# Last cross attention of a four-layer gated stack: six weight units in a ring, value products in halves, an unused product behind each half

## What is computed

```
q = (input @ Wq + bq).reshape(b, tq, H, D).transpose(0, 2, 1, 3)
kv = (encoded_features @ Wkv + bkv).reshape(b, tk, 2, H, D).transpose(2, 0, 3, 1, 4)
scores = jnp.einsum('bhqd,bhkd->bhqk', q, k) / math.sqrt(D)
attn = jax.nn.softmax(scores, axis=2)
out = jnp.einsum('bhqk,bhkd->bhqd', attn, v)
out = out.transpose(0, 2, 1, 3).reshape(b, tq, H * D)
return out @ Wo + bo
```

## Time and profile before

| | |
|---|---|
| median of three runs | 1382.56 us |
| the three runs | 1377.02, 1382.56, 1384.98 us |
| profiled execution | 1379.09 us |
| its span on the core | 1377.3 us |
| granted TensorE clock, mean of the span | 0.965 |
| PE / PEld busy | 91% / 65% |
| DVE / ACT / POOL busy | 71% / 68% / 54% |
| stage of the change (first scores to end of L1860's first addition) | 1261.7 to 1341.3 us |

### The profile page before, as it was taken

How to read it: one execution, slowest core, us unless ns; L and a number is a source line. 1 busy time by engine, 2 the same in 40 slices (tenths; PEclk the granted TensorE clock), 3 DMA queues, 4 the chain that set the end, 5 groups by cost and what they waited for, 6 DMA issues and landing times. The chain is left out here.

```text
span 1377.3 us, 44922 instructions
## 1 busy us (share of the span) xinstructions
PE 1253.2 (91%) x17964; PEld 893.7 (65%) x17964; DVE 975.1 (71%) x2481; ACT 934.4 (68%) x2297; POOL 742.6 (54%) x749
## 2 busy tenths in 40 slices
PE   6999978999999999999999999999868798997767
PEld 4777635676766777667667766667656666765444
DVE  3666648888888888888887888888743544544566
ACT  5777746677777777777767777777656555554771
POOL 3444438888878887878877778778710001004000
PEclk9999989999999999999999999999998898999799
DMA  4000033222225223422342234222302000000000
GB/s 198 1 1 1 1 111 72 66 62 60 60 63 143 60 61 84 124 56 65 79 125 52 62 80 121 57 62 70 81 2 100 0 1 27 1 0 1 1 1 16
DMA packets 68319, 76.95 MB, mean 56 GB/s; under 512 B 14864, under 2 KB 62992, under 8 KB 67600
## 3 DMA queue, kind: packets, MB, share of 16 engines
q1 hardware_dynamic: 68112, 74.07, 20.2%
HBM read 26.31 MB, written 0.52 MB: 19 GB/s over the span
## 5 line engine op out<-in xcount | busy, mean ns | idle before, releaser
L1047 POOL TENSOR_TENSOR arena<-arena,small 128x512 f32<-128x512 f32 x96 | 100.2, 1044 | 149.2 <-DVE small L930 149.2
L795 ACT ACTIVATE arena<-banks 128x512 f32<-128x512 f32 x96 | 57.4, 598 | 143.6 <-PE banks L653 143.4
L906 DVE TENSOR_TENSOR arena<-banks,rotary 128x512 f32<-128x512 f32 x192 | 131.6, 685 | 31.5 <-ACT arena L765 18.7
L1022 POOL TENSOR_TENSOR arena<-arena 128x512 f32<-128x512 f32 x96 | 122.9, 1280 | 36.3 <-DVE arena L908 36.2
L702 PE MATMUL banks<-arena 64*64 64x32 f32 x6144 | 112.5, 221 | 17.1 <-issue 9.6
L1027 POOL TENSOR_TENSOR arena<-arena 128x512 f32<-128x512 f32 x96 | 122.8, 1279 | 2.2 <-DVE arena L908 2.2
L702 PEld LDWEIGHTS banks<-arena 64*64 64x64 f32 x6144 | 100.4, 135 | 28.6 <-ACT arena L817 11.9
L503 POOL TENSOR_TENSOR arena<-arena,small 128x512 f32<-128x512 f32 x64 | 66.6, 1041 | 86.9 <-DVE small L437 86.9
L616 PE MATMUL banks<-slot,z 128*128 128x512 f32 x192 | 101.4, 610 | 7.4 <-DVE z L996 3.4
L717 PE MATMUL banks<-arena,slot 128*128 128x128 f32 x768 | 104.2, 279 | 2.1 <-ACT arena L825 1.9
L1034 POOL TENSOR_TENSOR arena<-arena,small 128x512 f32<-128x512 f32 x96 | 100.7, 1049 | 1.8 <-ACT small L805 1.8
(11 more groups left out here) (308 smaller groups left out, 3310.2 us busy)
## 6 DMA issues: line engine op xcount, KB each, us to landing
arena<-arena SPq DMA_DIRECT2D x576, 64.0 KB, 2.0
slot<-in_pack_dram SPq DMA_DIRECT2D x28, 339.5 KB
arena<-arena SPq DMA_DIRECT2D x288, 32.0 KB, 1.8
slot<-in_pack_dram SPq DMA_DIRECT2D x2, 2713.5 KB
slot<-in_pack_dram SPq DMA_DIRECT2D x1, 3333.0 KB
slot<-in_pack_dram SPq DMA_DIRECT2D x1, 2316.5 KB
slot<-in_pack_dram SPq DMA_DIRECT2D x4, 337.0 KB
slot<-in_pack_dram SPq DMA_DIRECT2D x7, 158.0 KB
```

What stands on the lines that cost most here:

```text
L906: e.tensor_tensor(rot, made, cos, ALU.mult)
L1022: e.tensor_tensor(m.rot_q[u % ROTS], m.rot_q[u % ROTS], m.sin_q[u % 2], ALU.add).then_inc(s["q_added"], 1)
L1047: e.tensor_tensor(p, p, stretch(m.local_small[u % 4][:, 16:24], SPAN), ALU.subtract).then_inc(s["lowered"], 1)
```

## The change

The weights of a unit go to one of six buffers in `slot0` (`RING3` = 6, 1024 columns each), whose own contents are no longer needed. The values' products of a pair of units are cut in their two halves i: one half behind the scores of unit n, the other behind those of n+1, later than before (`LAG3` = 3, plus one). Behind every half stands one product of the identity with `m.x[0]`, full in shape (128 rows, 128 columns of weights, 256 columns wide), into bank 7; nothing reads it. The sums of all b share bank 6, b even on the left and b odd on the right, so the first half for a new b waits until ScalarE has copied out the b before (`s3_kept` at b). `act_found3` stands one unit earlier in ScalarE's program (`KEEP3` = 3). ScalarE's wait for a free weights buffer is now on the pair of six units before.

```
-LAG3, KEEP3 = 2, 4
+RING3, LAG3, KEEP3 = 6, 3, 3
...
-def weights3(m, b, w):
-    part = (m.t_w[b][:, 0:1024], m.t_w[b][:, 1024:2048], m.t_w[b][:, 2048:3072], m.t_v[b])[w % 4]
+def weights3(m, n):
+    part = m.slots[0][:, n % RING3 * 1024:(n % RING3 + 1) * 1024]
     return part.rearrange("p (g i q) -> p g i q", g=2, i=NT)
+
+
+def found3(m, b):
+    return m.bank[6][:, b % 2 * N:(b % 2 + 1) * N]
...
-    for n in range(UNITS3 + LAG3):
+    for n in range(UNITS3 + LAG3 + 1):
...
-        if n >= LAG3 and (n - LAG3) % 2:
-            b, j, pair, w = unit3_of(n - LAG3)
-            out, vz = m.bank[6 + b % 2][:, b // 2 * N:(b // 2 + 1) * N], expanded_values(m, b)
+        if n >= LAG3 + 1:
+            v = n - LAG3 - 1 - (n - LAG3 - 1) % 2
+            i = (n - LAG3 - 1) % 2
+            b, j, pair, w = unit3_of(v)
+            out, vz = found3(m, b), expanded_values(m, b)
             e.wait_ge(s["s3_v"], 4 * b + j + 1)
-            if b < 2 and j == 0:
+            if b == 0 and j == 0:
                 e.wait_ge(s["p_kept_act"], 20)
                 e.wait_ge(s["p_kept_dve"], 12)
-            if b >= 2 and j == 0:
-                e.wait_ge(s["s3_kept"], b - 1)
-            for i in range(NT):
-                for g in range(GROUPS):
-                    made = e.matmul(out[32 * g:32 * g + 32, :], vz[:, i, g, j, :], weights3(m, b, w - 1 + g // 2)[:, g % 2, i, :],
-                                    start=(j == 0 and i == 0), stop=(j == 3 and i == NT - 1), skip_group_check=True)
-            made.then_inc(s["s3_o"], 1)
+            if b and j == 0:
+                e.wait_ge(s["s3_kept"], b)
+            for g in range(GROUPS):
+                made = e.matmul(out[32 * g:32 * g + 32, :], vz[:, i, g, j, :], weights3(m, v + g // 2)[:, g % 2, i, :],
+                                start=(j == 0 and i == 0), stop=(j == 3 and i == NT - 1), skip_group_check=True)
+            if i == NT - 1:
+                made.then_inc(s["s3_o"], 1)
+
+            e.matmul(m.bank[7][:, 0:N], m.ident, m.x[0], start=True, stop=True, skip_group_check=True)
...
-        p, least, total = weights3(m, b, w), m.s3_least[n % 4], m.s3_total[n // 2 % 4]
+        p, least, total = weights3(m, n), m.s3_least[n % 4], m.s3_total[n // 2 % 4]
         e.wait_ge(s["s3_least"], n + 1)
-        if j >= 2:
-            e.wait_ge(s["s3_o"], 4 * b + j - 1)
+        if n >= RING3:
+            e.wait_ge(s["s3_o"], (n - RING3) // 2 + 1)
```

More of the change, by code:

```diff
@@ L1505, in act_found3 @@
     e.wait_ge(s["s3_o"], 4 * b + 4)
-    e.activation(m.t_v[b][:, 0:N], m.bank[6 + b % 2][:, b // 2 * N:(b // 2 + 1) * N], ACT.Copy).then_inc(s["s3_kept"], 1)
+    e.activation(m.t_v[b][:, 0:N], found3(m, b), ACT.Copy).then_inc(s["s3_kept"], 1)
 def act_tail(e, s, m):
```

## The result

| | before | changed |
|---|---|---|
| median of runs | 1383.46 us (6 runs, 1375.1 to 1386.49) | 1437.6 us (6 runs, 1429.64 to 1449.51) |
| ratio, 95% interval | | 1.0397, 1.0358 to 1.0436 |
| profiled execution | 1379.09 us | 1437.31 us |
| its span | 1377.3 us | 1435.5 us |
| first scores to first addition to x | 1261.7 to 1340.9: **79.2 us** | 1265.7 to 1397.4: **131.7 us** |

The change makes the kernel 4% slower; the forecast was 1378.6 us with a range up to 1387. In all six executions of the changed kernel the mean granted clock is between 0.893 and 0.939, so the profiled one is no exception. Of the 58.2 us between the two spans 52.5 lie in the stage. 4.0 lie ahead of it and 1.7 behind; in the profiles of this study the stage begins anywhere between 1255.1 and 1269.4 us, with the same code ahead of it. From here on I therefore give the length of the stage beside the times.

A forecast was written before the change was run, and what follows sets the result against it. Bound before: the wait loop through the values' products, plus clock falls; afterwards TensorE at 2.24 us a unit. Loop +0.35 and tail -0.85 give -0.5 us from 1379.09: 1378.6 us, range 1370.5 to 1387.

The forecast's parts named there:

- The time of a unit: TensorE's loop at full clock: scores 1.07, half V 0.58, unused product 0.59, together 2.24 us a unit.
- A: Rival: changes of shape hidden, 1.74 us a unit, ScalarE binds the loop; 1368.6 us, chance 0.13.
- B: Rival: changes of shape half as dear with 32-wide groups, 2.0 us a unit; 1372.1 us, chance 0.12.
- C: Rival: changes into and out of four column groups paid in full, 2.54 us a unit; 1386.7 us, chance 0.10.
- TensorE as the bound: In the loop TensorE's 2.24 us a unit exceeds ScalarE's 1.81, so TensorE binds and is always busy.
- the free waits on copies: First half V of a b waits for the copy-out, which ends earlier: free by 0.8 us.
- the 1.7 us for its slow spell: Stage start: TensorE does half as much during a 3.4 us half-clock spell, losing 1.7 us.
- Its clock should then stay full: Loop: always busy, TensorE should keep the full clock, so units take 2.24 us.
- Start: Fifth unit's scores start at 1268.05; clock falls at 1268.2 for 3.4 us as before, costing 1.7 us.
- The reason given for the falls: Kernel before, loop: the clock falls because TensorE idles more than a microsecond in every turn.
- Rival D: Clock does not stay full in the loop; three 6.8 us spells cost 10.2 us more: 1388.8 us, chance 0.05.
- 18.9 us of cost against 6.5 us of low spells: Loop: unused products cost 32 x 0.59 = 18.9 us of TensorE; half-clock spells take some 6.5 us.

The follow-up runs named there:

- e2: Changed kernel plus seven unused full products ahead of its loop, where TensorE idled: 1372.29 us in one run, then 1381.38 us (ratio 1.0021).
- e13: Changed kernel's pieces, same amounts, reordered: scores of two units together, then half V, unused product, half V, unused product: 1371.8 us (one execution).
- e11: e2 plus one wait: TensorE waits ahead of unit 16's scores until unit 15's exponentials are done: 1413.85 us (one execution).
- e6: Changed kernel without unused products in the loop, but with seven ahead of it: 1373.08 us, ratio 0.9961.
- e1: Changed kernel without the unused product behind each half of the values' products: 1397.17 us, ratio 1.012.
- e15: Changed kernel's pieces, with both unused products of a pair moved behind the odd unit's half V: 1383.8 us (one execution).
- e3: Changed kernel with two unused full products behind each half of the values' products instead of one: 1400.07 us (one execution).
- e14: Changed kernel's pieces, same amounts, reordered: scores, whole V, scores, then two unused products: 1431.4 us (one execution).

## Why the prediction was wrong

**The time of a unit was right.** At the full clock e2 shows scores 1.06, half V 0.57, filler 0.63, together 2.26 us, against 1.07 + 0.58 + 0.59 = 2.24. The costs of changing shape taken from the earlier trace rows carry over to groups of 32. Rivals A, B and C fall with it: no change of shape is hidden or half as dear, and none costs 0.35. TensorE as the bound, ScalarE and VectorE waiting in each unit and the free waits on copies came as written; at the full clock the stage takes 77.3 us with the fillers ahead, where the forecast, less the 1.7 us for its slow spell, comes to 78.7 - 1.7 = 77.0.

**The step that failed** is "Its clock should then stay full", with its companion under *Start*: that the clock falls at 1268.2 "for 3.4 us as now". The low spell was given its old length because TensorE would be busy through it. The trace had the objection in it: the earlier trace rows shows spells of 6.8 us in which TensorE is busy 6.01 of 6.80 us, so low clock and busy went together already, and each of them ended after V and the scores of two units side by side, an order that the change takes away. In the chain of waits of the kernel before, the last rows ahead of the rise at 1281.9 are

```profile
1278.42 1.94 PE banks L1460 x16
1280.36 1.89 PE banks L1446 x16
```

with the two units of scores in 1.89 us, about half of the 3.90 us that they take one after the other in e13. I read the rise as the effect of being busy. One spell of 119 us took the place of the 1.7 us allowed. The reason given for the falls, that TensorE idles more than a microsecond in every turn, does not fit the rows either: from 1302.4 to 1333.2 it is idle 10.24 of 30.80 us, 1.10 us ahead of nearly every V, and the clock is 1.00 throughout.

**Rival D** named the right mechanism, a clock that does not stay full, but priced it by today's spells, 10 us. As a level that this loop can't leave it is 50 us; and "against it: never idle" was no argument.

**The skill's rule** that activity lifts the low clock (the Trainium skill, "TensorE: Matmul & The Clock Gate", Part 1) was cited as agreeing. The trace of the changed kernel does not agree if activity means TensorE's busy time: 116.00 of 116.00 us busy at 0.50. The falls came behind idle time (2.6 us in the changed kernel, 2.1 us in e11), but the rows with idle time at 1.00 say that idle time alone does not decide when. The Trainium skill's rule on weight loads (the same page, Part 3), which pointed to rival C, did not decide anything.

**The fillers** were judged by the wrong sum. I set 18.9 us of cost against 6.5 us of low spells. At the full clock one filler a unit costs 0.63 us and holds a level that e6, without it, holds as well for most of the loop; at the lower clock it costs 1.15 us and lifts nothing. Two lift it, but their own time takes back nearly all of the gain: the stage is 95.6 us against 97.4 without any (e1).

## What to carry to other kernels

A busy TensorE is not a fast TensorE: read the granted clock beside the busy time, and for each rise and fall note what ran before it, in which shapes; a change of order can lock a loop at the lower level. Where products use a part of the rows, put products of other row groups next to them and keep tile sizes equal, so that they run at once, gather the other products in longer stretches (e15 against the changed kernel), and close idle gaps ahead of a loop rather than inside it, if the loop cannot lift the clock by itself. Compare lengths of a stage when the parts ahead of it vary by more than the effect.

## What the runs showed of the hardware

- The loop of the changed kernel, never idle, keeps the level of the clock at which it is entered: 1.00 for 70 us (e2) and 0.50 for 116 us, with the same instructions. Other orders, as busy, were lifted (e3, e13, e15).
- One idle time of 2.1 us took it down for 63 us and more (e11). Idle times of 0.96 us (e6, twice) and 1.10 us (before, in each turn from 1307 on) left it at 1.00.
- The order of equal pieces decides whether it is lifted: stage 73.5 us (e13), 81.4 (e15), 124.5 (e14), 131.7 (changed).
- Products of 64 rows and of 32 rows on different rows did not overlap (1.15 us each); 32 with 32 did, at no cost.
- Changing the array between row groups, column groups and full costs 0.52 us in a unit of three changes at the full clock (2.26 less 1.74).
